# Retention in chunks of 64 with tiles of pairs of heads, a scan for the states, and modulation rows in column tiles

## The reference

```python
x = L0_attn_x                                     # (4, 512, 256)
mod = (_silu(c) @ wmod).reshape(4, 6, 1, -1)      # sa, ca, ga, sb, cb, gb
ga = sign(ga) * max(|ga|, 0.25); gb likewise
h = _layernorm(x) * (1 + ca) + sa
# retention, 16 heads of 16, gamma per head:
q, k, v = h@wq+bq, h@wk+bk, h@wv+bv
scores = einsum('bhnd,bhmd->bhnm', q, k) * where(n >= m, gamma ** (n - m), 0)
ret = einsum('bhnm,bhmv->bhnv', scores, v)
norm = (ret - mean) * rsqrt(var + 1e-5) * gn_w + gn_b   # mean, var over a head's positions and columns
x = x + ga * ((silu(h@wg+bg) * norm) @ wo + bo)
h = _layernorm(x) * (1 + cb) + sb
# experts: top 2 of h@gate_kernel, softmax of the two as weights
x = x + gb * sum_e combine_e * (silu(h@w0_e) * (h@w1_e)) @ wo_e
```

## Time and profile before

| | us |
|---|---|
| median of 3 runs | 470.18 (468.26 to 473.09) |
| the profiled execution's own time | 468.83 |
| its span, first to last instruction | 466.8 |

### The profile page before, as it was taken

One profiled execution on the slowest core, in us unless ns is written; L12 is line 12 of the kernel. 1 busy time (PEld: TensorE's weight loads), 2 busy tenths in 40 slices (PEclk: granted clock), 3 DMA queues, 4 the chain that ended last, 5 costly groups with the idle time before them and its releaser, 6 DMA issues.

```text
span 466.8 us, 8611 instructions
## 1 busy us (share of the span) xinstructions
PE 418.6 (90%) x2160; PEld 283.9 (61%) x2161; DVE 302.4 (65%) x766; ACT 184.4 (39%) x346; POOL 245.3 (53%) x170
## 2 busy tenths in 40 slices
PE   2989999999699997997799978999999999999990
PEld 2445546565366554553466644788888888788870
DVE  4398756785475836788465734877677776777750
ACT  3252255334332534422112112455566555655530
POOL 3013621655318361655216453677777777777752
PEclk9998999999999999999799998999999999999996
DMA  7659971103511043003443684244333443334322
GB/s 242 210 190 374 373 260 46 35 1 127 102 45 34 0 183 90 0 0 115 149 125 62 168 262 116 58 87 86 68 68 68 80 88 71 68 72 87 56 22 22
DMA packets 34779, 50.32 MB, mean 108 GB/s; under 512 B 4924, under 2 KB 21700, under 8 KB 34760
## 3 DMA queue, kind: packets, MB, share of 16 engines
q1 hardware_dynamic: 24520, 36.17, 26.4%
q0 software_dynamic: 8176, 13.65, 13.2%
q10 hardware_dynamic: 2064, 0.28, 0.4%
HBM read 31.93 MB, written 18.16 MB: 107 GB/s over the span
## 4 chain that ended last, share of the span: by engine, by line
PE 58%; DVE 15%; DMA 10%; issue 8%; POOL 5%; ACT 1%; SPq 1%; DVEq 1%; POOLq 0%; ACTq 0%
PE ps L1498 11%; PE ps L1328 7%; PE ps L1482 6%; PE ps L1479 6%; PE ps L1478 6%; DMA out_dram<-wg_s,qd 4%; PE ps L1364 3%; POOL routed L500 3%; PE ps L1266 3%; PE ps L1490 3%; DVE sm L913 2%; PE ps L1285 2%; DMA routed<-h,idx 2%; PE ps L1469 2%; PE ps L1464 2%
## 5 line engine op out<-in xcount | busy, mean ns | idle before, releaser
L538 POOL TENSOR_TENSOR w_lo<-we,w_hi 128x1024 fp32r<-128x1024 f32 x30 | 74.1, 2471 | 25.1 <-ACT w_hi L707 25.1
L1498 PE MATMUL ps<-we,qx 128*128 x312 | 75.9, 386 | 1.2 <-ACT qx L692 0.8
L1498 PEld LDWEIGHTS ps<-we,qx 128*128 128x128 f32 x312 | 57.7, 191 | 19.5 <-issue 12.2
L692 ACT COPY qx<-ps 128x512 f32<-128x512 f32 x39 | 22.9, 587 | 113.3 <-PE ps L1490 113.3
L1328 PE MATMUL ps<-qx,kT 128*128 128x512 f32 x128 | 62.0, 606 | 4.6 <-DVE sm L913 4.4
L548 POOL DMA_INDIRECT out_dram<-wg_s,qd x30 | 47.1, 1570 | 32.3 <-DMA out_dram<-wg_s,qd 11.4
L629 ACT ACTIVATE qx<-qT,hmask 128x128 f32<-128x128 f32 x128 | 39.2, 389 | 43.1 <-PE ps L1328 38.1
L913 DVE TENSOR_TENSOR sm<-ps,dmask 128x512 f32<-128x512 f32 x64 | 43.3, 689 | 12.1 <-PE ps L1328 11.6
L458 POOL TENSOR_TENSOR qx<-qT,hmask 128x1024 f32<-128x1024 f32 x16 | 30.3, 1895 | 30.4 <-PE ps L1328 15.6
L500 POOL DMA_INDIRECT routed<-h,idx x32 | 31.4, 981 | 25.6 <-DVE idx L1029 17.1
L1168 DVE TENSOR_TENSOR w_halves<-we,w_halves 128x1024 fp32r<-128x1024 f32 x30 | 38.9, 1296 | 7.1 <-ACT w_halves L707 7.0
(11 more groups left out here) (208 smaller groups left out, 770.7 us busy)
## 6 DMA issues: line engine op xcount, KB each, us to landing
rowbuf<-routed SPq DMA_DIRECT2D x39, 260.5 KB, 2.9
we<-in_ffn_w_kernel_dram SPq DMA_DIRECT2D x16, 512.0 KB, 10.0
we<-in_ffn_wo_kernel_dram SPq DMA_DIRECT2D x8, 512.0 KB, 10.2
routed<-z SPq DMA_DIRECT2D x9, 260.5 KB, 3.3
xs<-in_attn_x_dram SPq DMA_DIRECT2D x4, 512.0 KB, 13.1
h<-gb_dram SPq DMA_DIRECT2D x16, 128.0 KB, 6.0
out_dram<-xs SPq DMA_DIRECT2D x4, 512.0 KB, 3.0
we<-in_wmod_dram SPq DMA_DIRECT2D x1, 1536.0 KB, 7.2
```

What stands on the lines that cost most here:

```text
L538: g.tensor_tensor(w_lo[1], expert_up(e, 1), w_hi[1].bitcast(F32), ALU.subtract)\
L1498: last = mm(down_ps, eit[s % 2][:, k, :], weights(e, 2 * FT * F + k * D, D), start=k == 0, stop=k == KF - 1)
```

## The change

- Chunks of 64 positions (8 of them). The queries are no longer expanded by 8: ACT writes, besides qT, two copies of them straight from PSUM, one with the even heads and one with the odd heads of each pair (`qeo`, `queries`). The decayed queries `qd` are made by POOL (`decay_q`) instead of DVE.
- Scores: per chunk, half of the features and pair j, one matmul with contraction over 32 rows, 64 weight columns and 128 moving columns; the four pairs j are four row tiles and go to four banks; even chunks go to partitions 0 to 63, odd ones to 64 to 127. One bank then holds the scores of 4 chunks for one pair, and DVE masks a bank in one instruction (8 per batch instead of 16).
- Values: contraction over 64 rows, 32 weight columns, 64 moving columns, 128 matmuls per batch; even and odd chunks accumulate in different banks (`ret[r]`).
- States: all 7 parts by 56 matmuls (contraction 64, 32 by 32) into two tail banks, masked by 4 DVE instructions, and one scan over 448 elements gives all states; state times query are 56 matmuls (contraction 32, 32 weight columns, 64 moving columns).
- The front ring has 4 banks (it takes over the two score banks), the scores are items of it; the tail ring keeps 2.
- All loops over batches are written out; the orders of PE, DVE, ACT and POOL are new: rows of v and k ahead of g, `out_rows` behind `rows_v`, all scores of half 0, `from_states`, `turn_h2`, scores of half 1, router, values. `scatter(b)` moves to batch b + 2 of POOL's order, and `scatter(2)` behind `group_power(3)`. `rank(b)` moves into batch b + 2.
- Setup: the modulation rows are column tiles, 4 vectors of 256 in 4 partition groups of 32; `features(0)` on ACT stands behind the wait for the small vectors and for the parity mask. The table of decays for the scan lies in expert 6's weights, so `load_expert(6)` waits for the last scan.

The core of the diff:

```diff
+CH = 64
+NCH = S // CH
+PAIRS = 4
+SETS = 2
...
-        sc = [ps[2], ps[3]]
-        front = Ring(FRONT, [ps[4], ps[5]], sem("front_full"), ...
+        front = Ring(front_items(), ps[2:6], sem("front_full"), ...
...
@@ sync
+            sp.wait_ge(state_ready, B)
+            load_expert(E - 2)
             sp.wait_ge(tab_ready, 2)
             sp.wait_ge(h2_free, B - 1)
...
@@ gpsimd
-            for b in range(B - 1):
-                group_power(b)
-                expand_q(b + 1, 0)
-                modulate(b)
-                expand_q(b + 1, 1)
-                scale_wo(b + 1)
-                expand_q(b + 1, 2)
-                add_bias(b + 1)
-                expand_q(b + 1, 3)
-                scatter(b, range(NC))
-                scatter_done(b)
+            for b in range(B):
+                p = b - 1
+                decay_q(b, 0)
+                if p >= 0:
+                    group_power(p)
+                decay_q(b, 1)
+                if p >= 1:
+                    scatter(p - 1, range(NC))
+                    scatter_done(p - 1)
+                if b == 0:
+                    pool.wait_ge(wo_in, 16 * 2)
+                scale_wo(b)
+                if b + 1 < B:
+                    first_power(b + 1)
+                if p >= 0:
+                    modulate(p)
+                add_bias(b)
+            group_power(B - 1)
+            scatter(B - 2, range(NC))
+            scatter_done(B - 2)
...
@@ scalar
+            normed(0)
             act.wait_ge(modT_ready, 2)
-            features(0)
             act.wait_ge(small_in, SMALL)
...
+            act.wait_ge(par_ready, 3)
+            for b in range(B):
+                p = b - 1
+                features(b)
+                queries(b)
+                keys(b, 0)
+                if p >= 0:
+                    group_normed(p)
+                keys(b, 1)
+                gate(b, 0)
+                gate(b, 1)
+                if b + 1 < B:
+                    normed(b + 1)
+                if p >= 0:
+                    h2_features(p)
+                    top_tanh(p)
...
@@ vector
+            def states(b):
+                dve.wait_ge(qd_ready, FT * b + FT)
+                for r, n in enumerate(("stE", "stO")):
+                    dve.wait_ge(tail.full, tail.filled(b, n))
+                    for ft in range(FT):
...
+                        ins = v.tensor_tensor(stm[:, ft, :, r:NCH - 1:2].rearrange("p d t -> p t d"), src[:, 0:m, :],
+                                              blk32[:, :].unsqueeze(1).broadcast_to([P, m, 2 * DH]), ALU.mult)
...
+                v.tensor_tensor_scan(flat[0], flat[1], flat[2], 0.0, ALU.mult, ALU.add).then_inc(state_ready, 1)
...
+                states(b)
+                if not last:
+                    shift(b + 1)
+                if last:
+                    tile_columns(0)
+                if p >= 0:
+                    second_norm(p)
+                masks(b, 0)
+                if last:
+                    table_rows(0)
+                gates(b)
+                masks(b, 1)
+                if p >= 0:
+                    take_logits(p)
+                    choose_top(p)
+                    choose_places(p)
+                    choose_weights(p)
...
@@ tensor
+            def scores(b, u, pairs):
...
+                                last[j] = mm(front.bank(b, f"s{u}{j}")[CH * r:CH * r + CH, at:at + 2 * CH],
+                                             kT[32 * j:32 * j + 32, ft, c * CH:(c + 1) * CH],
+                                             qeo[32 * j:32 * j + 32, ft, c, :, :].rearrange("p q n -> p (q n)"),
+                                             start=True, stop=True, skip_group_check=True)
+            def from_states(b):
...
+                            mm(ret[r][32 * j:32 * j + 32, at:at + CH], state[32 * j:32 * j + 32, ft, :, c - 1],
+                               qd[32 * j:32 * j + 32, ft, c * CH:(c + 1) * CH], start=c < 3 and ft == 0, stop=False,
+                               skip_group_check=True)
+            def values(b, u):
+                wait(pe, front.drains(b, f"s{u}{PAIRS - 1}"))
...
+                                    last = mm(ret[r][32 * j:32 * j + 32, at:at + CH],
+                                              vx[CH * r:CH * r + CH, tb, v0:v0 + 32],
+                                              sm[CH * r:CH * r + CH, u, j, t, ft, q, :],
+                                              start=False, stop=q == 1, skip_group_check=True)
...
+                state_parts(b)
+                scores(b, 0, range(PAIRS))
+                if final:
+                    firsts(0)
+                from_states(b)
+                if final:
+                    fold(0)
+                if p >= 0:
+                    turn_h2(p)
+                scores(b, 1, (0, 1))
+                scores(b, 1, (2, 3))
+                if p >= 0:
+                    router(p)
+                values(b, 0)
+                values(b, 1)
```

More of the change, by code:

```diff
@@ L357, in _ @@
             sp.wait_ge(gb_out, 16)
-            load_expert(E - 2)
             load_expert(E - 1)
@@ L1388, in rank @@
             def rank(b):
-                wait(pe, tail.free(b, "rank"))
+                wait(pe, tail_free(b, "rank"))
                 pe.wait_ge(msk_ready, b + 1)
```

893 lines of the change are left out of this document (427 added, 466 removed).

## The result

The changed kernel takes 478.75 us (median of 4 runs, 477.89 to 480.26) beside 470.78 for the kernel before (4 runs): a ratio of 1.0155, 95% interval 1.0112 to 1.0198. It is slower by 1.6%; forecast were 446 us. On two other chips the changed kernel took 481.3 and 480.9 us, the kernel before 482.2 and 471.0, so the ratio there was 0.998 and 1.019: what differs from chip to chip is mostly the kernel before. Single executions that lie over 1.5% above the fastest of their kernel are left out of the ratios but not of the medians, so the two can differ by up to 1%.

A forecast was written before the change was run, and what follows sets the result against it. TensorE (PE), busy 90% of the 466.8 us span, was taken as the bound. 34.9 us won by the end of the values, less 9 given back and 1.5 for code fetching, gave 470.2 - 24.4 = 446 us, range 430 to 468.

The forecast's parts named there:

- The price p of an instruction: Small matmuls on PE: 20 ns for each of 608 instructions per batch, between bounds of 13.5 and 27 ns.
- for fetching straight code: Whole kernel: 1.5 us of the 25.9 us won on the span set aside for fetching straight code.
- The instruction counts and array times of each part: PE per batch: state parts 2.2, scores 1.3 twice, from_states 2.2, values 5.1, together 12.3 us against 26 before.
- The wait before the output rows: PE's wait for gA falls from 3.3 to about 1.3 us in batches 2 and 3, to nothing in batch 1.
- the rival that had them take turns: Row tiles on PE take turns, scores 6.9 us each half, from_states 5.9: 480 us, chance 0.12.
- The wait for h2: PE at turn_h2, three times: h2 ready at 32.7 us after the last values, a wait of 3.8 us.
- The clock: After each wait for h2 PE runs at 1.2 GHz for 3.4 us, which costs 1.7 us more.
- The start: Start of the kernel: q starts at 21.9 us instead of 19.82, state parts at 38.2.
- What is given back: Behind batch 3's values: later scatter(2) delays the third row load, PE waits 8 to 9 us; 9 us lost.
- hidden, with 6 us to spare: load_expert(6) starts 26.5 us into batch 3, needs 10 to 13 us, PE wants it at 46: no cost.
- Average holds, p 27: Rival for the small matmuls on PE: 27 ns an instruction, 12 us more, 458 us, chance 0.22.
- Small tiles don't hold the clock: Rival: turn_h2 to the values at 1.2 GHz, 9 us longer instead of 1.7, three times: 468 us, chance 0.10.

The follow-up runs named there:

- f_spread: Changed kernel with the expert weights loaded behind the values of batches 0, 1 and 2 instead of in batch 0; 0.988 of the kernel before.
- f_four: Changed kernel with turn_h2 and router between value halves, later fill_gb(3), expert 6, batch 2 fills and store, and spread weight loads; 449.1 us, 0.945 of the kernel before.
- g_busy: f_spread with 5 or 8 useless dense matmuls in place of PE's wait for h2 in batches 1 to 3; 0.987 of the kernel before.
- a_late6: Changed kernel with expert 6 loaded only behind h2 of batch 3; 0.9935 of the kernel before.
- a_probe: Changed kernel with three extra stretches of unused matmuls ahead of the state parts of batches 0, 1, 2; 128 records every 6.48 us in batch 0, 3.46 in batch 1.
- f_quiet: Changed kernel with the gate fills and store of batch 2 and expert 6 issued only behind h2 of batch 2; 1.0179 of the kernel before.
- after: The profiled execution of the changed kernel as it is, 477.89 us.
- g_power: f_spread with POOL's scale_wo, first_power and power of the second norm ahead of scatter_done; 0.985 of the kernel before.

## Why the prediction was wrong

The end of each batch's values and what comes behind, as forecast and as measured:

| us | forecast | changed kernel | f_spread | f_four |
|---|---|---|---|---|
| batch 0 ends | 52.4 | 63.0 | 51.6 | 53.3 |
| batch 1 lasts | 42.3 | 45.2 | 42.5 | 42.1 |
| batch 2 lasts | 43.8 | 50.5 | 50.9 | 44.6 |
| batch 3 lasts | 46.5 | 55.3 | 52.0 | 48.9 |
| from there to the end | 257.4 | 262.2 | 262.1 | 260.6 |

**The price p of an instruction, and one price for all: wrong, the step that failed.** I took 20 ns between 13.5 and 27 from bursts of at most 32 instructions and multiplied. That is a price of the array alone; for the supply of instructions the sum has no term but 1.5 us "for fetching straight code". The burst is even cheaper than its lower bound: 112 state parts in 1.16 us are 10 ns each. But behind it stands a supply of 256 instructions in 3.5 us at best and 6.5 beside bulk transfers, 27 to 51 ns for a matmul instruction: from the upper of the two values between which I chose to twice that. That is a rate of the instruction stream, not of the array, so it appears as pauses and in no duration. Measured were eight pauses of 21.5 us behind packets of q8, out of a miss of 29 us at the end of batch 3's values (214.0 for 185.0). Batch 0 was forecast right to 1 us as soon as the weights didn't run beside it (f_spread), batch 1 as well, in part by luck: the values of batch 0 took 3.3 us of PE instead of 5.1, which covers the pause of 0.96 and the wait of 0.88 for DVE's masks that weren't in the sum. With the loads moved, the miss of 29 us shrinks to 12.

The row that could have warned stood on the page of the kernel before, among its queues (packets, MB, share):

```profile
q8 instruction: 8, 0.13, 0.1%
```

I didn't read it. The change takes PE from 286 matmul records per batch to some 710, each with a weight load; 608 records with their loads are 4.75 blocks per batch, by estimate 16 us at 3.5 us each, where I had 12.3, and 31 us in batch 0 at 6.5 each (measured there from the first state part to the last value: 24.7 us, for 14.2 forecast).

The change also writes PE's loop over the batches out, and no run parts the two. In the kernel before no packet of q8 starts between 112.7 and 219.9 us, while its loop does batches 2 and 3; in the changed kernel 12 start between 108.2 and 214.0. Whether a hardware loop over the same small matmuls would have paid for its instructions only once stays untested.

**The instruction counts and array times of each part: right.** State parts at 38.34 (38.2 forecast), values 3.7 us (5.1), scores of a half 1.2 at full clock (1.3), but 2.3 to 2.9 behind a wait; the small groups of a batch are 11.0 to 13.3 us together (12.3). The scan was right in two batches (1.09 us for 1.0) and took 2.3 and 2.1 us in batches 0 and 2. The wait before the output rows of batches 2 and 3 came as forecast (1.5 us for 1.3). Row tiles together: right; the rival that had them take turns was wrong in its mechanism, and that its 480 us lie beside the measured 478.75 is luck.

**The wait for h2: right in place, too small in size.** 4.8, 5.5 and 4.6 us were forecast as 3.8 each. In batch 2 of f_spread h2 comes 6 us later after the start of the batch than summed (133.0 - 94.1 = 38.9 for 33). Half of it is that state parts start at +25.4 us instead of +22.3: the first q projections run at low clock, and two small matmuls of the rank are in front. The other half is POOL's queue: second_norm's power stands behind scatter_done, and I had named only DVE's queue there.

**The clock: right as a consequence of waits, mis-sized.** I allowed 1.7 us for each wait for h2, from one row. The stage from turn_h2 to the values of batch 2 is at 0.51 over its whole 11.9 us, and costs at least the 2.4 that g_busy took off. In the changed kernel these stages last 11.2, 12.0 and 11.9 us, where 10.8 were summed: the miss in the clock is partly hidden by cheaper values. The pauses of supply bring it down at further places (0.72 to 0.84 by stage, for 0.95 to 1.00 in the earlier trace rows). Mean over the run 0.881 for 0.972.

**The start: right.** q at 21.8 (21.9), state parts within 0.2 us.

**What is given back: 9 forecast, 15.3 measured.** The wait for the third row load is there, 10.8 us. SP and PE in order of time, answering:

```profile
233.33 1.76 SPq L401 DMA_DIRECT2D h<-gb_dram  x4
235.85 0.35 SPq L414 DMA_DIRECT2D rowbuf<-routed  x1
...
242.55 0.69 PE L1522 MATMUL ps<-ident,rowbuf 128*128 128x128 f32 x2 [10.82 <-DMA rowbuf<-routed]
243.03 3.62 PE L1527 MATMUL ps<-we,xn 128*128 x4
```

Behind the wait the first two groups of matmuls run at low clock (3.6 us for 1.9 the one, 2.1 us in all), and the two later waits for routed rows are 6.9 us together for 4.1 before: 10.8, 2.1 and 2.8 make 15.7 of the 16.1 between the two kernels up to the first tile with split weights (72.8 us after the values before, 88.9 now). I had counted the clock and left out the second chain, from the last router over the scatter to the next row loads. The transfer of expert 6 was "hidden, with 6 us to spare" as a transfer; it is one of those that stand beside the pause of 5.9 us, though moving it alone (a_late6) left 5.2.

**The rivals.** None had it. "Average holds, p 27" (458 us) named the quiet rate by accident, from a row that has another cause. "Small tiles don't hold the clock" gave the symptom that is there, for a wrong cause: the same tiles keep it at 1.00 behind dense work (g_busy). The least distance of 25 ns between starts, which the Trainium skill gives ("TensorE: Matmul & The Clock Gate", Part 1), does not bind here: in bursts between tiles the starts are 10 ns apart, 112 in 1.16 us.

## What to carry to other kernels

Count PE's instructions, weight loads included, and set them against the supply: 256 in 3.5 us in this kernel with no other transfers, 6.5 beside bulk loads. A stretch of PE work with less than 14 ns for an instruction (27 for a matmul with its load; 3.46 us / 256 and / 128 in a_probe) outruns it, however cheap each is. Its mark is idle time by "issue" in the middle of equal matmuls, the same count apart. Idle time by "issue" ahead of a new group can be a plain wait whose releaser isn't named, as DVE's scan was here. Place bulk transfers beside stretches of long matmuls, not beside short ones: that alone turned a 2% loss into a 1% gain here, and with the waits reordered it became about 5%.

## What was unexpected of the hardware

- The supply of instructions to PE: one block of 256 in 3.46 us with DMA share 0.02, in 6.48 us with 1.06 (a_probe), and single pauses of 5.1 to 5.9 us beside 128 KB fills, a store and an expert load, 1.0 without them (f_quiet). The 16 KB packet itself takes 0.9 to 1.4 us in each of these places; beside bulk transfers it starts later. Why it does stays open.
- Tiles in different rows and columns of the array overlap fully even in one PSUM bank when each has its own 32 partitions: 96 instructions of 512 columns in 10.5 us. Starts of small matmuls in different tiles come 10 ns apart on average (112 in 1.16 us).
- The granted clock over the same small tiles is 0.50 to 0.66 behind a wait of 4.1 to 7.2 us (after, f_spread, g_power), and 0.82 and 1.00 behind dense work (g_busy).
- Left open: whether the small matmuls in a hardware loop would run without the pauses; why the scatter's move alone gives the kernel before 3% on one chip, and why the kernel before differs by 2.4% between chips (470.8 and 482.2 us) while the changed one does not (478.8 to 481.3).
